# A decoder layer on one core: the recurrence's division by logarithm, exponential and one Newton step, and scaling ahead of rounding on ScalarE

## The reference

```python
x = x + attention(layernorm(x))        # 16 heads of 32, one shared key/value head, rope, 8-bit grid for K and V,
                                       # windows of 128 in steps of 64: sigmoid(scores) / sum, linearly blended
x = x + wkv(w, u, layernorm(x), ctx)   # k = layernorm(x), v = ctx, a scan over the 256 tokens:
#   y = (A * p + E * vt) / (A * q + E),  then p, q decay by w and take in the token
x = x + ffn(layernorm(x))              # bit_linear: rows rounded to 8 bits by their largest value, weights to -1, 0, 1
#   h = silu(gate) * up;  h = rms_norm(h) * ln_weight;  out = bit_linear(h, w_down)
```

## Time and profile before

| | us |
|---|---|
| median of 3 runs | 1213.55 (1212.55 to 1216.14) |
| profiled execution, its own time | 1216.07 |
| its span, first to last instruction | 1214.8 |
| busy in the span: PE / DVE / ACT / POOL | 965.8 / 986.7 / 663.9 / 406.5 |
| mean granted TensorE clock, share of full | 0.945 |

### The profile page before, as it was taken

How to read it: one execution, slowest core, us unless ns; L and a number is a source line. 1 busy time by engine, 2 the same in 40 slices (tenths; PEclk the granted TensorE clock), 3 DMA queues, 4 the chain that set the end, 5 groups by cost and what they waited for, 6 DMA issues and landing times. The chain is left out here.

```text
span 1214.8 us, 26234 instructions
## 1 busy us (share of the span) xinstructions
PE 965.8 (80%) x10555; PEld 624.3 (51%) x10644; DVE 986.7 (81%) x1669; ACT 663.9 (55%) x1162; POOL 406.5 (33%) x496
## 2 busy tenths in 40 slices
PE   4774645888888897979888888888888888888747
PEld 2442624555555555555646464656464655555323
DVE  4757549588888888898989798979797989888775
ACT  2342623574747566665747374747565657474514
POOL 2110011242525243424342424242433425252513
PEclk9997676999999999999999999999999999999969
DMA  7993502002020202020201111020202020201000
GB/s 254 358 377 97 184 1 55 9 1 81 1 81 1 81 1 81 1 82 0 67 15 54 29 37 45 19 63 18 64 2 80 2 81 1 82 1 37 1 17 18
DMA packets 42346, 75.22 MB, mean 62 GB/s; under 512 B 8208, under 2 KB 22000, under 8 KB 41072
## 3 DMA queue, kind: packets, MB, share of 16 engines
q1 hardware_dynamic: 34912, 59.52, 15.6%
q10 hardware_dynamic: 6384, 10.34, 2.3%
q0 software_dynamic: 928, 3.68, 0.8%
HBM read 55.17 MB, written 18.35 MB: 61 GB/s over the span
## 5 line engine op out<-in xcount | busy, mean ns | idle before, releaser
L464 PE MATMUL bank<-w_up_gate,qT 128*128 128x512 bf16 x993 | 223.9, 382 | 22.8 <-ACT qT L657 20.6
L1175 POOL TENSOR_TENSOR work<-junk,lnw 128x512 f32<-128x512 f32 x128 | 165.9, 1313 | 112.2 <-DVE junk L1008 112.2
L380 PE MATMUL bank<-wide,early 32*128 32x192 f32 x2048 | 111.6, 358 | 75.8 <-ACT arena L631 52.1
L464 PEld LDWEIGHTS bank<-w_up_gate,qT 128*128 128x128 bf16 x1024 | 99.3, 98 | 135.5 <-ACT qT L657 20.1
L417 PE MATMUL bank<-wo_sb,wide 128*128 128x512 f32 x256 | 129.4, 664 | 39.8 <-DVE wide L912 39.8
L631 ACT ACTIVATE arena<-bank 128x384 f32<-128x384 f32 x256 | 104.9, 496 | 77.5 <-PE bank L380 77.3
L380 PEld LDWEIGHTS bank<-wide,early 32*128 32x128 f32 x2048 | 91.4, 201 | 98.6 <-ACT arena L631 72.1
L364 PE MATMUL bank<-wide,wq_sb 128*128 128x256 f32 x512 | 119.5, 388 | 8.7 <-DVE ext L785 8.7
L657 ACT COPY qT<-bank 128x1024 bf16<-128x1024 bf16 x16 | 16.2, 1012 | 199.3 <-PE bank L442 199.3
L487 PE MATMUL bank<-w_down,work 128*128 128x512 bf16 x454 | 115.3, 393 | 12.2 <-issue 6.7
L1008 DVE TENSOR_TENSOR junk<-bank,junk 128x512 f32<-128x512 f32 x128 | 85.1, 685 | 48.5 <-PE bank L464 25.5
(11 more groups left out here) (148 smaller groups left out, 1701.2 us busy)
## 6 DMA issues: line engine op xcount, KB each, us to landing
x_norm_T<-sums ACTq DMA_DIRECT2D x8, 1024.0 KB, 8.6
wide<-x_norm_T SPq DMA_DIRECT2D x16, 512.0 KB, 5.3
rows<-in_x SPq DMA_DIRECT2D x16, 512.0 KB, 4.7
ctx_T<-in_ctxT SPq DMA_DIRECT2D x16, 512.0 KB, 4.0
out<-rows SPq DMA_DIRECT2D x32, 256.0 KB, 2.3
rows<-in_x SPq DMA_DIRECT2D x4, 1024.0 KB, 5.6
wide<-in_x SPq DMA_DIRECT2D x4, 1024.0 KB, 7.1
w_up_gate<-in_wdT SPq DMA_DIRECT2D x4, 1024.0 KB, 11.2
```

Of the source, the lines that this page charges most:

```text
L380: last = te.matmul(bank[j][:, kt * QW:(kt + 1) * QW], k_pair[head, n, kt * P:(kt + 1) * P], q[head, c, kt * BLK:kt * BLK + QW], start=n == ...
L464: last = te.matmul(bank[4 + k % 4][:, :], qT[:, c, t * P:(t + 1) * P], w_up_gate[:, m, c, cols], start=c == 0, stop=c == NC - 1)
L1175: ge.tensor_tensor(hid_w[:, t, cols], hid[:, n % 2, :], lnw[:, cols], op=ALU.mult).then_inc(z_set.sem, 1)
```

## The change

The reciprocals on VectorE go. In their place ScalarE takes Ln of the joined denominators into the free part of `state` (`wkv_logs`) and Exp of the negative (`wkv_inverses`), r; VectorE multiplies den by r (`refine`), GpSimd the numerator by r (`outputs`), and VectorE forms (den * r - 2) * (num * r) (`quotient`), which is the Newton step with its sign turned; the residual therefore subtracts. The scalings ahead of both roundings move to ScalarE as Copy with a scale (`scale_tokens`, `scale_hidden`); VectorE keeps the roundings (`wkv_round`, `hidden_round`).

The orders of all four engines change with it. `gate_up(f, 1, 0)` and `hidden(f, 0, 2)`, `hidden(f, 0, 3)` move from the end of a round to the start of the next; `wkv_keys`, `exps` and `key_steps` run in the round of their own sequence; the rounding of w_up moves from round 0 into round 1 on VectorE, ahead of its second `rope`; the sums of |w_gate| on ScalarE come behind `set_keys(0)`, those of |w_up| behind `exps(0)`.

```diff
@@ scalar_program
+        def wkv_logs(w, k):
+            cs = slice(2 * k, 2 * k + 2)
+            se.wait_ge(joined.sem, joined.at(w))
+            se.activation(state[:, cs, DEN, 1:], GG[:, cs, DEN, :], ACT.Ln).then_inc(den_logged.sem, 1)
+
+        def wkv_inverses(w, k):
+            cs = slice(2 * k, 2 * k + 2)
+            se.wait_ge(den_logged.sem, den_logged.at(w, k))
+            se.activation(state[:, cs, DEN, 1:], state[:, cs, DEN, 1:], ACT.Exp, scale=-1.0).then_inc(
+                den_inverted.sem, 1)
+
+        def scale_tokens(w):
...
+                se.activation(tok_f[:, t, :], tok_f[:, t, :], ACT.Copy, scale=amax[:, 1, t:t + 1]).then_inc(
...
+        def scale_hidden(f, t):
+            se.wait_ge(z_set.sem, z_set.at(f, NF * t + NF - 1))
+            se.wait_ge(h_scale.sem, h_scale.at(f, 4 * t + 3))
+            se.activation(hid_w[:, t, :], hid_w[:, t, :], ACT.Copy, scale=col[t]["qscale"]).then_inc(h_scaled.sem, 1)
@@ vector_program
-        def divide(w, k):
+        def refine(w, k):
             cs = slice(2 * k, 2 * k + 2)
-            ve.wait_ge(joined.sem, joined.at(w, 2 * k + 1))
-            ve.reciprocal(GG[:, cs, DEN, :], GG[:, cs, DEN, :]).then_inc(inv_set.sem, 1)
+            ve.wait_ge(den_inverted.sem, den_inverted.at(w, k))
+            ve.tensor_tensor(GG[:, cs, DEN, :], GG[:, cs, DEN, :], state[:, cs, DEN, 1:], op=ALU.mult).then_inc(
+                refined.sem, 1)
+
+        def quotient(w, k):
+            cs = slice(2 * k, 2 * k + 2)
+            ve.wait_ge(refined.sem, refined.at(w, k))
+            ve.wait_ge(y_part.sem, y_part.at(w, k))
+            ve.scalar_tensor_tensor(GG[:, cs, NUM, :], GG[:, cs, DEN, :], 2.0, GG[:, cs, NUM, :],
+                                    op0=ALU.subtract, op1=ALU.mult).then_inc(y_set.sem, 1)
...
-            for t in range(NT):
-                ve.tensor_scalar(tok_f[:, t, :], tok_f[:, t, :], inv[:, t:t + 1], None, ALU.mult).then_inc(
-                    f_scaled.sem, 1)
...
-            ve.tensor_scalar(hid_w[:, t, :], hid_w[:, t, :], col[t]["qscale"], None, ALU.mult).then_inc(
-                h_quant.sem, 1)
...
+            if i == 1:
+                weight_mean(UP)
+                for k in range(NC):
+                    round_weights(UP, k)
@@ pool_program
         def outputs(w, k):
             cs = slice(2 * k, 2 * k + 2)
-            ge.wait_ge(inv_set.sem, inv_set.at(w, k))
-            ge.wait_ge(joined.sem, joined.at(w, 2 * k + 1))
-            ge.tensor_tensor(GG[:, cs, NUM, :], GG[:, cs, NUM, :], GG[:, cs, DEN, :], op=ALU.mult).then_inc(y_set.sem, 1)
+            ge.wait_ge(joined.sem, joined.at(w))
+            ge.wait_ge(den_inverted.sem, den_inverted.at(w, k))
+            ge.tensor_tensor(GG[:, cs, NUM, :], GG[:, cs, NUM, :], state[:, cs, DEN, 1:], op=ALU.mult).then_inc(
+                y_part.sem, 1)
```

More of the change, by code:

```diff
@@ L510, in tensor_program @@
             if do_f:
-                hidden_T(f, 0)
+                gate_up(f, 1, 3)
             if do_b:
@@ L514, in tensor_program @@
             if do_f:
+                hidden_T(f, 0)
+            if do_b:
+                scores(b, 1)
+            if do_f:
                 down(f, 0, 0)
             if do_b:
-                scores(b, 1)
                 scores(b, 2)
@@ L522, in tensor_program @@
                 scores(b, 3)
+                dens(b, 0)
+                dens(b, 1)
             if do_f:
@@ L551, in tensor_program @@
                 gate_up(w, 0, 3)
-                gate_up(w, 1, 0)
+            if do_b:
+                wkv_keys(b)
     def scalar_program(se):
@@ L693, in scalar_program @@
                 squares(f, 1, 1)
+                scale_hidden(f, 0)
                 silu(f, 1, 3)
-            if do_w:
-                exps(w)
+                squares(f, 1, 2)
+            if do_b:
+                probs(b, 0)
             if do_f:
-                squares(f, 1, 2)
                 squares(f, 1, 3)
@@ L728, in scalar_program @@
                 silu(w, 0, 3)
+            if do_b:
+                exps(b)
+            if do_w:
                 squares(w, 0, 2)
@@ L1057, in vector_program @@
             if do_f:
+                hidden(f, 0, 2)
+                hidden(f, 0, 3)
+            if do_b:
+                rope(b, 0)
+            if do_w:
+                values(w)
+            if do_f:
                 hidden(f, 1, 0)
@@ L1060, in vector_program @@
                 hidden(f, 1, 1)
-            if do_b:
-                rope(b, 0)
+            if i == 1:
+                weight_mean(UP)
+                for k in range(NC):
+                    round_weights(UP, k)
             if do_f:
                 hidden_scale(f, 0)
-                hidden_quantise(f, 0)
                 hidden(f, 1, 2)
-                hidden(f, 1, 3)
             if do_b:
                 rope(b, 1)
+            if do_f:
+                hidden_round(f, 0)
+                hidden(f, 1, 3)
             if do_w:
-                values(w)
                 scan(w, 0)
@@ L1077, in vector_program @@
                 scan(w, 1)
+                join(w)
+            if do_f:
+                hidden_round(f, 1)
+                output(f, 0)
             if i == 0:
@@ L1081, in vector_program @@
                     round_weights(GATE, k)
-            if do_f:
-                hidden_quantise(f, 1)
             if do_w:
-                join(w)
-                divide(w, 0)
-                divide(w, 1)
-            if do_f:
-                output(f, 0)
-                output(f, 1)
+                refine(w, 0)
+                refine(w, 1)
+                quotient(w, 0)
             if do_b:
@@ L1093, in vector_program @@
                 blend_windows(b, 1)
+            if do_w:
+                quotient(w, 1)
+            if do_f:
+                output(f, 1)
             if do_w:
@@ L1102, in vector_program @@
                 wkv_quantise(w)
+                wkv_round(w)
             if do_b:
@@ L1105, in vector_program @@
                 att_norm(b)
-            if i == 0:
-                weight_mean(UP)
-                for k in range(NC):
-                    round_weights(UP, k)
             if do_w:
```

94 lines of the change are left out of this document (52 added, 42 removed).

## The result

The changed kernel takes 1245.07 us (median of 4, 1243.51 to 1249.37) against 1213.58 for the kernel before beside it: a ratio of 1.0262, 95% interval 1.023 to 1.0294, slower by 31.5 us where 10 were forecast. The profiled execution has a span of 1242.5 us (1214.8 before) and an own time of 1243.82. Executions over 1.5% above the fastest of their kernel count as slow and ratios leave them out; only experiment 10 had such, two of its four.

What follows compares the result with a forecast made beforehand. No engine is full: a ring of waits, ScalarE pacing the front half. Start 3.0, rounds 4.2, round 15's front half 1.7 and end 1.5 make +10.4 us, 1223.5 from 1213.55; range 1199 to 1240 (8 in 10).

Steps and rivals of the forecast that it cites:

- The direction: Whole kernel: slower by 10.4 us, to 1223.5; slower as an outcome got 0.55.
- The clock: TensorE's granted clock in steady rounds: no term in the sum, forecast as 0 us.
- rival C: TensorE's clock: waits spread otherwise, no round slow any more, 17 us given back, 1206.5 us; chance 0.28.
- C's own sign: Ahead of `attention_out`: the wait stays under 2.45 us, and `attention_out` takes 7.13 in all rounds.
- The steady ring: Steady round, a ring of waits with no engine full: front half +1.7, back half -1.4, together +0.3 us.
- The third inverse: Front half on ScalarE: `attention_out` comes 4.15 us after it starts; four new instructions ahead of it add 2.4 us.
- Rival A: Back half: ScalarE becomes late too, with 0.1 us to spare over 10.8; 1237.5 us, chance 0.21.
- The products and quotients: VectorE, steady round: two products and two quotients at 0.75 each, 3.0 us; net -7.0 us on that engine.
- waiting ahead of `refine`: Steady round: VectorE waits about 5 us for the exponentials there, a sign that the forecast is right.
- ScalarE's prices: Steady round: Ln and Exp 0.60 each, scalings of 2048 columns 1.91 each, eighth table load 1.28; 8.7 us more busy.
- Start: Before round 1's scores: w_up's rounding moves ahead of the second `rope`, scores at 199.5 against 196.49, +3.0 us.
- End: After the last rounds: `down` copies behind the exponentials +0.9, last hidden scaling +0.6, together +1.5 us.

Runs made afterwards that it cites:

- experiment 10: Changed kernel with the last blends (windows 2 and 3) ahead of the residual and nums of window 3 ahead of wkv_back: 1294.6 us, ratio 1.0567.
- experiments 1: Changed kernel with the 16 transposes of hidden_T(f, 0) done twice, in the wait behind the first scores group: 1224.28 us, ratio 1.0086.
- 2: Changed kernel with hidden_T(f, 0)'s transposes doubled and 3 and 5 unused matmuls before and behind tokens_T: 1216.68 us, ratio 1.0021.
- experiment 4: Changed kernel with the reciprocal back on VectorE in place of the division by logarithm, orders and scalings as changed: 1199.07 us, ratio 0.9883.
- Experiments 9: Kernel before with only the division changed, plus last blends ahead of the residual and nums of window 3 ahead of wkv_back: 1262.45 us, ratio 1.0371.
- 8: Changed kernel with nums of window 3 ahead of wkv_back on TensorE: 1248.41 us (2 runs), ratio 1.0283.
- experiment 5: Kernel before with only the new division, orders and scaling as before except both outputs ahead of the quotients on VectorE: 1294.63 us, ratio 1.0665.
- experiment 11: Changed kernel with w_up's rounding right behind round 1's keys on VectorE, its sums ahead of exps(0): 1244.96 us, ratio 1.0237.

## Why the prediction was wrong

The direction was right, the size a third of the true one. By its own steps:

- **The clock failed, and it is most of the error.** The sum took the share of slow rounds over unchanged; rival C only asked whether fewer would be slow, and watched one place, the wait before `attention_out`. I wrote that "PE's waits are spread otherwise now, with `hidden_T` and `dens` in them", and drew from it only a gain. That wait did shrink, from 2.45 to 1.74, and `attention_out` did take 7.13 in all steady rounds but one: C's own sign, without C's gain. But the clock now fell behind the 2.05 us that `hidden_T` (1.07) leaves open behind the first scores group, and around the tokens. 15.1 us forecast as 0, and 1.6 more in round 15; experiments 1, 2 and 10 show it from both sides.
- **The steady ring was right.** Front 31.38 (31.6 forecast), back 31.35 (31.3), round +0.1 for +0.3. The third inverse holds the front half, 4.17 us ahead of `attention_out`: in experiment 10 VectorE's queue was shortened and nothing was gained, and in experiment 4 the four Ln and Exp went and 1.63 were gained. Rival A did not come about: 0.80 us of wait for PE stand before the first sigmoids' table load.
- **The products and quotients were mis-sized, and what stands behind them was not looked at.** Four at 0.75 were forecast, from a row without POOL beside it. They measure 2.28 for two, 1.62 and 0.68, as `outputs` and the weighting run at the same time. `keys_grid`, taken as unchanged, takes 2.3 to 2.6 for its first two steps instead of 1.72, beside GpSimd again (445.07, 638.98), and a round's busy time on VectorE falls by 5.0 us instead of 7.0. The forecast of "about 5 us" of waiting ahead of `refine` held (5.10), but behind it VectorE is full to the last blend, some 11.2 us from `refine` to `attention_out`. In a steady round this just fits under ScalarE, whose copies for `down` stand between its inverses. In round 1 there are no such copies: the third inverse starts 7.2 us after the table load of the recurrence's exponentials (222.24 to 229.42) instead of 9.0, and VectorE's queue decides: `attention_out` starts 6.77 us after that inverse instead of 4.17. Its front half takes 37.3 instead of 34.5: the round +3.3 for +0.3. Experiments 9 and 10 show the queue as a cause (in 10 the 6.77 fall to 5.06), 8 excludes TensorE's order as the whole of it, and experiment 5 shows what it costs in orders that have no copies there in any round.
- **ScalarE's prices held**: two logarithms and two exponentials near 0.6 each, the scaling 2.0 (1.91 forecast), the eighth load 1.28. L649 starts 0.02 us after its load ends, and the load 0.02 after the sigmoids. The Trainium skill, "ScalarE: Activation LUTs", section "What ACT_TABLE_LOAD costs", adds about 1380 ns of drain to a load; none shows in any of the runs.
- **Start** +2.4 for +3.0, by the mechanism given. **End** +2.6 for +1.5; which of the parts there is longer was not tested. The slower clock stands on both sides: on `gate_up` after (8.77 at 1149.35), on `attention_out` before (8.83 at 1114.57).

What stays open: why one round loses its clock behind a wait of 2.05 and the next, with the same instructions and waits, does not. The runs show how often, not which: the second scores group is slow in eight of the fourteen rounds of the changed kernel, in four in experiment 4, eleven in 8 and twelve in 10. Nor does the length of the wait alone decide: `attention_out` loses the clock behind 2.45 in eight rounds of the kernel before, and behind 2.92 in two of experiment 8.

## What to carry to other kernels

When TensorE waits in every round, treat each wait that a change lengthens as a term of its own, with the price of the matmuls behind it at half clock: here a wait that grew from 1.19 to 2.05 us cost up to 1.5 us in eight of fourteen rounds, and 0.9 us of useless transposes in it bought back 21 us over the run. Moving work to an idle engine gains nothing by itself; look at who stands behind the new hand-overs in the queue of the engine that was relieved, and price operations from rows with the same neighbours running. Test the parts of a change apart: here the orders and scalings gained 14 us and the division lost 46.

## What the runs showed of the hardware

- Two halves with the same instructions and waits differ by 1.5 to 1.7 us, all of it in the matmuls behind a wait, with 0.50 to 0.81 of the full clock over their stretch (596.63 to 599.57 and 436 to 445). Between the scores groups the kernel before waited less at a time and lost no clock: no group of rounds 2 to 15 takes more than 1.58. Its PE:

```profile
580.41 1.67 PE L487 MATMUL bank<-w_down,work 128*128 128x512 bf16 x7 [0.16 <-issue]
583.27 1.58 PE L380 MATMUL bank<-wide,early 32*128 32x192 f32 x32 [1.19 <-ACT arena L631]
586.57 1.58 PE L380 MATMUL bank<-wide,early 32*128 32x192 f32 x32 [1.71 <-ACT arena L631]
```

- VectorE's product of 128x512 takes 1.14 to 1.18 us beside GpSimd and the quotient 1.62, against 0.68 for the quotient alone; GpSimd's pair of weightings takes 3.12 beside the quotient, which reads two operands from SBUF, and 2.24 beside the residual, which reads one from PSUM and keeps its 0.7. The Trainium skill, "GPSIMD Engine Reference", section "Specifications", has the two share SBUF interfaces, with contention for VectorE's instructions of two SBUF inputs; the trace agrees.
- A sum over the partitions on GpSimd started 4.7 us after its input was ready, 5.8 after other work of that engine (experiment 11), without a wait that the trace names. In the changed kernel, where GpSimd had been idle for 11.1 us, the same instruction starts 0.14 us after its input (181.56 to 181.70).
